# Two gather stages of a graph network kernel: the gathering engine waits for a different finisher of its buffer

## The reference, cut to what matters

```python
# layer 0
agg = jax.ops.segment_sum(x[src], dst, num_segments=x.shape[0])
h = agg + x                     # then two dense layers with a normalization between
# layer 1 (messages: fixed maps of x[src], weighed by four edge attributes and a radial weight)
src = node_in[edge_src]
agg = jax.ops.segment_sum(messages, edge_dst, num_segments=node_in.shape[0])
```

## Time and profile before

| | |
|---|---|
| median of 3 runs | 3287.35 us (3279.5 to 3292.2) |
| profiled execution | 3315.14 us |
| span in that execution, first to last instruction | 3313.5 us |
| granted TensorE clock, mean share of full speed | 0.927 |
| busy share: PE, DVE, ACT, POOL | 84%, 55%, 43%, 56% |
| first gather stage, first gather to last addition | 58.6 to 1095.5 us |
| second gather stage, first gather to last addition | 1706.6 to 2950.6 us |

### The profile page before, as it was taken

One profiled execution on the slowest core, in us unless ns is written; L12 is line 12 of the kernel. 1 busy time (PEld: TensorE's weight loads), 2 busy tenths in 40 slices (PEclk: granted clock), 3 DMA queues, 4 the chain that ended last, 5 costly groups with the idle time before them and its releaser, 6 DMA issues. The chain is left out here.

```text
span 3313.5 us, 54301 instructions
## 1 busy us (share of the span) xinstructions
PE 2769.0 (84%) x15515; PEld 2310.4 (70%) x15515; DVE 1823.2 (55%) x5496; ACT 1410.1 (43%) x3910; POOL 1844.2 (56%) x1958
## 2 busy tenths in 40 slices
PE   1888898899888899699957787888877778769998
PEld 1667777778777788588846555566666667659998
DVE  5742223577665566545547445466555565555555
ACT  4012222244222455346544366577645565532222
POOL 5666666666666155456666555566666566624343
PEclk9999999899998999899978899899978888879999
DMA  7244444666665377345542333334435555442222
GB/s 220 77 114 124 119 122 125 193 198 207 202 204 181 124 231 224 115 132 168 163 147 82 107 92 99 103 107 117 116 108 154 145 146 143 135 137 76 76 82 66
DMA packets 269039, 453.82 MB, mean 137 GB/s; under 512 B 74642, under 2 KB 194173, under 8 KB 267670
## 3 DMA queue, kind: packets, MB, share of 16 engines
q1 hardware_dynamic: 184386, 232.20, 23.5%
q0 software_dynamic: 77376, 211.49, 22.3%
q10 hardware_dynamic: 7006, 6.97, 0.8%
HBM read 338.67 MB, written 111.83 MB: 136 GB/s over the span
## 5 line engine op out<-in xcount | busy, mean ns | idle before, releaser
L2644 POOL DMA_INDIRECT g_got<-xm_d,idx x750 | 730.9, 975 | 502.1 <-PE ps L2233 216.2
L921 POOL DMA_INDIRECT g_got<-xn_d,idx x654 | 650.1, 994 | 385.9 <-issue 185.7
L2233 PE MATMUL ps<-g_hotw,g_got 128*128 128x96 f32 (+11 forms) x3000 | 428.4, 290 | 86.2 <-issue 63.1
L2233 PEld LDWEIGHTS ps<-g_hotw,g_got 128*128 128x128 f32 x3000 | 398.5, 200 | 130.0 <-issue 129.1
L1305 PEld LDWEIGHTS ps<-g_hot,g_got 128*128 128x128 f32 x2616 | 348.1, 203 | 80.1 <-issue 71.3
L1305 PE MATMUL ps<-g_hot,g_got 128*128 128x120 f32 (+4 forms) x2616 | 360.2, 286 | 46.0 <-issue 29.6
L2702 ACT ACTIVATE g_hotw<-g_hot,g_wr 128x16 f32<-128x16 f32 (+8 forms) x1308 | 299.2, 309 | 52.9 <-DVE g_hot L632 40.1
L3011 PE MATMUL ps<-g_half 128*125 128x512 f32 x400 | 205.1, 660 | 77.0 <-ACT g_half L2673 50.2
L1112 DVE TENSOR_TENSOR g_ring<-g_ring,ps 128x40 f32 (+8 forms) x327 | 68.8, 210 | 334.6 <-remote 168.9
L2852 DVE TENSOR_TENSOR g_ring<-g_ring,ps 128x140 f32 (+9 forms) x375 | 129.8, 346 | 146.8 <-DMA p_xin<-in_x 47.9
L1440 PE MATMUL ps<-g_hT,g_w 128*128 128x250 f32 x800 | 199.9, 394 | 10.8 <-issue 8.6
(11 more groups left out here) (427 smaller groups left out, 5454.3 us busy)
## 6 DMA issues: line engine op xcount, KB each, us to landing
h_d<-gin_hid SPq DMA_DIRECT2D x23, 1000.0 KB
gin_hid<-h_d SPq DMA_DIRECT2D x23, 1000.0 KB
job_in<-jobs_d SPq DMA_DIRECT2D x54, 258.0 KB
g_got<-xm_d,idx POOLq DMA_INDIRECT x750
p_z<-z_d SPq DMA_DIRECT2D x49, 224.0 KB
g_got<-xn_d,idx POOLq DMA_INDIRECT x654
q_d<-g_qo SPq DMA_DIRECT2D x25, 250.0 KB
g_wqkv<-q_d SPq DMA_DIRECT2D x25, 250.0 KB
```

The costliest lines, as they stand in the source:

```text
L921: landed.start(e.indirect_dma_start(got[:, k % (2 * GB), :], None, xn_d[0:N, :], bass.IndirectOffsetOnAxis(ap=idx[:, HT + k:HT + k + 1], a ...
L2233: mm = e.matmul(to, rows[j][:, c * P:(c + 1) * P], hotw[:, j, c * w:4 * w].unsqueeze(1).broadcast_to([P, r, n]), start=(j == 0), stop=(j = ...
L2644: landed.start(e.indirect_dma_start(got[:, 2 * (n % GB) + j, :], None, xm_d[0:N, :], bass.IndirectOffsetOnAxis(ap=idx[:, at:at + 1], axis= ...
```

## The change

In both stages the gather of a pair waits for the addition of the pair that had its slot, and no longer for that pair's sums. Nothing else differs; the count waited for is the same pair's.

```diff
                     def gather(k):
                         if k % 2 == 0:
-                            summed.wait(e, k // 2 - GB, "sums")
+                            added.wait(e, k // 2 - GB, "add")
                             e.sem_inc(s_held["Pool"], 1)
...
                     def gather(n):
-                        summed.wait(e, n - GB, "sums")
+                        added.wait(e, n - GB, "add")
                         e.sem_inc(s_held["Pool"], 1)
```

## The result

The changed kernel takes 3437.45 us in the median of three runs (3432.1 to 3443.3), where the kernel before took 3287.35: a ratio of 1.044, with a 95% interval from 1.041 to 1.047. That is 150 us, and far outside the predicted 3270 to 3308. The profiled execution took 3432.1 us. The head of its page answers to the earlier trace rows: every engine has the same number of instructions, and the span grew by 117 us (the profiled execution of before was itself 28 us over its median).

The account below looks back on a forecast made before the run. TensorE was taken to bound both gather stages, with POOL running ahead. All terms cost 0 us, so the sum was 0: 3315.1 us for the profiled execution, 3287 us for the median, range 3270 to 3308 us.

Parts of the forecast that it names:

- What bounds the kernel: Both gather stages: TensorE is fullest, POOL runs ahead and waits; a gather costs time only if TensorE waits for rows.
- How much time the ring holds: Both gather stages: a release may come 27.0 us (first) or 32.8 us (second) after its sums before TensorE waits.
- how late the release becomes: Both stages: additions up to four or eight pairs behind, 12.3 or 24.6 us in the first stage, 13.2 in the second.
- My 6.9 us: Landing of a gather's rows after its issue: taken as at most 6.9 us, from the second stage's sixth gather.
- Cost: 0: First stage's end and second stage's longest hold: the later gathers still come early enough, so no time is lost.
- The "issue" of the earlier trace: TensorE's unnamed idleness before the sums, 29.6 and 63.1 us: waits for rows could hide there, together at most 92.7 us.
- The ring rival: Both stages: slots held longer act like a smaller ring; 0.5 us of excess costs 28 us, giving 3315 us; chance 0.08.
- POOL as the bound: Gather stages: each pair newly pays 0.51 us, first stage up to 86 us too much, giving 3373 us; chance 0.02.
- The third rival: Later gathers disturb transfers or TensorE's "issue" pieces less; a quarter of 92.7 us gives 23 us, 3264 us; chance 0.07.
- What would show it: Signs in the later trace: POOL's idle time ends on additions, "issue" stays near 29.6 and 63.1 us, stages 1037 and 1244.
- pair 57: Second stage, longest hold: its gather starts 13.3 us later, at 1891.2, right after the hole and with that of pair 58.
- two signs of being wrong: Gaps before a pair's first product, its gather issued under 7 us before; or POOL without addition waits while TensorE idles.

Follow-up runs that it names:

- clumps of six: Kernel before, with POOL waiting only ahead of every sixth pair, for the sums of the last slot it then refills: ratio 1.150.
- ring of 6 (7): Kernel before, with POOL waiting for the sums of six pairs later, so 6 pairs are used in the first stage, 7 in the second: ratio 0.994.
- pauses of 2.6 us: Changed kernel, with POOL also waiting ahead of every fourth pair until the pair before has landed: ratio 1.054.
- Pauses of about 0.8 us: POOL waits for a landing between two gathers: changed kernel, after six gathers, 1.041; kernel before, after six 1.022, after four 1.040.

## Why the prediction was wrong

**What bounds the kernel.** TensorE is the fullest engine and POOL isn't waited for: right, and right still. The step that failed is the sentence drawn from it, "a gather costs time only if TensorE has to wait for its rows". It set the price of the whole change, since everything after it counts rows. The runs show a second price: gathers issued one after another for over some 8 to 10 us slow TensorE, rows or no rows. It came to 150 us, with every pair's rows landed at least 2.1 us before their use.

**How much time the ring holds, and how late the release becomes.** These held, with room to spare. The landing has a row now, 2.23 us behind the end of the issue in the place shown above. My 6.9 us came from one gather and was no bound: by the semaphores of the kernel before, a pair's second gather landed 1.8 us behind the end of its issue in the median, but 9 of the first stage's 327 pairs took longer than 6.9 us, up to 9.4. The Trainium skill, "DMA: Bandwidth & Descriptors", section "Anatomy of one DMA — SWDGE (gpsimd) path", gave an estimate of 2.3 us for this transfer, and the place shown agrees. Half the ring costs nothing, so "Cost: 0" was right for lateness.

**The "issue" of the earlier trace rows.** I read it as the place where waits for rows could hide, found it short and left it. It was the mark of the stalls: most of it comes in the middle of a pair's matmuls, where the program has no wait (breaks of over 0.3 us there sum to 115 us with the change), and it is in the kernel before too (84 us). The table above finds the same behaviour there, in fewer us.

**The rivals.** The ring rival named the right sign for a wrong reason. The rule cited with it, of the Trainium skill, "Perfetto Trace Analysis", section "Optimization Strategy", that a recurring gap on the full engine can mean too few buffers, doesn't hold for these gaps: with six pairs in place of twelve TensorE's idleness in the two stages fell from 400 to 358 us (ratio 0.994). POOL as the bound didn't come. The third rival, "later gathers disturb less", had the right mechanism, gathers that disturb TensorE's "issue" pieces, with the wrong sign: I asked how much later the gathers come and not how they bunch. Additions come in clumps and pairs behind the sums, so POOL works off a backlog and can't be stopped by a stall.

**What would show it.** POOL's waits and pair 57 came as foreseen, and the lengths of the stages did not. Of the two signs of being wrong, late gathers in front of a pair did not come; POOL without any wait while TensorE idles did, from 938.6 to 945.9 us in the rows above. I had named it as a sign and not seen that it could be a cause. The landing was not what I misjudged, and VectorE's order not in the way I meant: that additions come late and in clumps made no rows late, but it gave POOL its backlog.

**The size.** Idleness: 68 us in the profiled execution, 67 of it net between 8 us into a burst and 2 us after its end. The other 49 us are TensorE's longer busy time under a lower granted clock (0.91 and 0.87, before 0.94 and 0.89). That the lower clock follows from the stalls is argued from windows like that at 938 us; no run changed the clock alone.

**Open.** What in the chip holds TensorE up isn't in the traces. Nothing points to the loading of instructions: of the 257 idle stretches of over 0.3 us that are "issue" in the two stages with the change, 3 end within 0.5 us after the end of one of the 207 transfers of instructions there, where chance would give 11. VectorE seems to be held too. In the timeline of the clumps of six, in the first burst cut up above:

```profile
628.86 0.26 PE L1306 MATMUL ps<-g_hot,g_got 128*128 128x112 f32 x1 [0.36 <-issue]
...
633.50 0.21 DVE L1113 TENSOR_TENSOR g_ring<-g_ring,ps 128x56 f32 x1 [9.83 <-remote]
```

By the order of the sums the addition at 633.50 needs the pair that TensorE ended at 629.12 and the one before it; it starts 4.4 us later, after a wait whose end the profile gives to no engine ("remote"). In the next burst an addition, at 654.10, comes 8.5 us after the sums that it needs. Also open is why the ring of 6 (7) is 0.6% faster than the kernel before. And it isn't separated whether the length of a burst counts by itself or only that POOL goes on while TensorE stands: the pauses of 2.6 us, which cut the bursts and left POOL untied, made rows late as well.

## What to carry to other kernels

A wait is also a brake: before it is moved to a later or lumpier event, ask what the engine behind it will do when the one it used to follow stands still. Count bursts as well as rates; here the same gathers cost 0 to 15%, depending only on what releases them. If a buffer really must be released by a late event, a second wait on the full engine's progress, two pairs later here, gives the brake back.

## What the hardware showed that was not expected

With gathers issued by POOL every 1.26 us, TensorE began to stall some 8 to 10 us into the row, in the middle of matmul groups without a wait, for up to 1.9 us at a time at the sums of the changed kernel, and ran again about 2 us after the row's end. It was idle for 8 to 11% of a row's first 8 us and for 38 to 57% of the time beyond 10 us. Pauses of about 0.8 us did not end it. The DMA engines' share was 0.32 in one such stretch and 0.88 in another, so their load isn't the measure of it.
